# A four-layer graph kernel: how its first inputs arrive, and the order of its first products

## The chip, the cores and the metric

The kernel runs on one core of a Trainium2 chip. The metric is the device time of one execution in microseconds (us), the median of several. A core has a matrix engine (TensorE, PE), whose weight loads are shown apart (PEld), a vector engine (VectorE, DVE), a scalar engine (ScalarE, ACT), a general engine (GpSimd, POOL) and a sync engine (SP). Each engine works through its own list of instructions in order and waits for the others at semaphores. Transfers are issued by SP and by ACT, each on its own queue; both queues are served by the same 16 DMA engines. Matrix products are written to PSUM, eight banks of 128 x 512 numbers, and are read from there by DVE and ACT.

## What is computed

Four layers follow one another on 64 graphs of 128 nodes with 256 features. Each normalises its input, computes something of it and adds that to x:

```python
h = jnp.maximum(_layernorm(x, axis=-1), 0.0)
x = x + _L0_gnn_ref(h, adj, Wq, Wk, Wv)   # linear attention, relations normed by row
...                                       # L1: graph attention, L2: graph convolution, L3: 8-head attention

def _L0_gnn_ref(neuron_states, adjacency, Wq, Wk, Wv):
    q = jnp.einsum('bnd,ed->bne', neuron_states, Wq)
    k = jnp.einsum('bnd,ed->bne', neuron_states, Wk)
    v = jnp.einsum('bnd,ed->bne', neuron_states, Wv)
    rel = jnp.einsum('bnd,bmd->bnm', q, k)
    rel = adjacency.T[None, :, :] * rel
    rel = rel / jnp.linalg.norm(rel, axis=2, keepdims=True)
    return jnp.einsum('bnm,bmd->bnd', rel, v)
```

Only the first layer's start is touched here.

## The kernel before

All 64 graphs stay in on-chip memory (`xs`); the layers run one after the other, each over 32 pairs of graphs. In the first layer the two weights of query and key are multiplied once: q k^T is h (Wq^T Wk) h^T, so one product of the weights, `MM`, replaces two per pair. Each 32-bit operand of the large products is split into a rounded high part (written by ACT) and the rest, the low part (written by DVE from PSUM and the high part), and a product is the sum of high x high, high x low and low x high; such a `split_product` for one pair is 12 matmuls (L410).

The order on each engine is written out by hand, first a prologue, then `step(p, b)` for each pair. For one pair the work goes: moments, mean and variance (DVE L135 to L150, `statistics`), the reciprocal root (POOL L161), the normalised pair (`normalise` on DVE L706 for pairs 0 and 1, POOL from pair 2), its transposes on PE (`turn`, L172, into bank HT), high part on ACT (`relu_high`, L613 and L569), low part on DVE (`low_part`, L749), the t product with the split weights (`t_product`, L410, needs the low part), the values with the split value weight (`values`, L410; it needs the value bank to be read out by `low_v` of the pair before, DVE L766), `relation` (L494), the mask on DVE (L756), `relation_outputs` (L441) and the update of x (L773).

The prologue before: SP issues Wq, the second pair of graphs (2 and 3), Wv, the adjacency, W1, a small vector, the fifth pair and five weights of later layers. ACT issues the first pair (0 and 1, 256 KB), Wk, the four graphs of pairs 2 and 3 (512 KB, `x_third`), three bias rows, beta and the two small vectors bq and bk, whose elements lie apart in memory. PE runs six matmuls on zeros (L515), the product of the weights (L519, x8 in the profile, since a 32-bit matmul shows as two records), the first pair's transposes, the turn of Wv (L501), `t_product(0)`, `turn(1)`, the adjacency's transpose, `values(0)`, `relation(0)` and the turn of W1. On DVE the product of the weights is split by one subtraction of 128 x 512 (L783) and the turned Wv by another (L788); `degrees` sums the adjacency's rows.

Of the kernel before, what the change touches and what calls it, by code (L numbers as in the profile page):

```python
# [7 lines left out]
F32 = mybir.dt.float32  # L8
F32R = mybir.dt.float32r
ALU = mybir.AluOpType  # L10
# [4 lines left out]
def gnn_stack_kernel(nc, x, adj, w):  # L15

    GRAPHS, N, D = x.shape
# [11 lines left out]
    with ExitStack() as ctx:  # L30
# [3 lines left out]
        def sem(name):  # L34
            return ctx.enter_context(nc.semaphore(name))
# [133 lines left out]
        def transposes(pe_ps, src=xn):  # L169
            for c in range(C):  # L170
                for g in range(2):
                    ins = nc.tensor.transpose(pe_ps[:, c * 2 * N + g * N:c * 2 * N + (g + 1) * N],  # L172
                                              src[:, g, c * 128:(c + 1) * 128], ident[:, :])
            return ins
# [24 lines left out]
        qk_loaded, wv_loaded, w1_loaded, adj_loaded = sem("c_qk_loaded"), sem("c_wv_loaded"), sem("c_w1_loaded"), sem("c_adj_loaded")  # L199
        rows_loaded = sem("c_rows_loaded")  # L200
        raw_loaded = [sem(f"c_raw_loaded{k}") for k in range(5)]
        c_plain = sem("c_plain")
        c_zeros, c_ident, c_mhalf = sem("c_zeros"), sem("c_ident"), sem("c_mhalf")
        m_done, turned, wa_done, adjT_done = sem("c_m_done"), sem("c_turned"), sem("c_wa_done"), sem("c_adjT_done")
        plain_adjT_done = sem("c_plain_adjT_done")
# [11 lines left out]
        def chunks(weight):  # L217
            return weight.rearrange("(c p) n -> p c n", p=128)

        def as_chunks(ps):  # L220
            return ps[:, :].rearrange("p (c n) -> p c n", c=C)
# [205 lines left out]

        HT, TT, VV, RR, RT, OO = bank[0:6]
        AP = OO
        plain = wide[:, 0, 0:3, :].rearrange("p i n -> p (i n)")  # L430

        l0_v_ready, l0_relm_low, l0_out_done = v_ready, relm_low, out_done
# [12 lines left out]
        with nc.Block() as block:  # L445
            @block.sync
            def _(sp):
                sp.dma_start(wq0[:, :, :], chunks(w["L0_gnn_Wq"])).then_inc(qk_loaded, 16)
                sp.dma_start(xs[:, 2:4, :], x[2:4, :, :].rearrange("g n d -> n g d")).then_inc(x_second, 16)
                sp.dma_start(wv0[:, :, :], chunks(w["L0_gnn_Wv"])).then_inc(wv_loaded, 16)  # L450
                sp.dma_start(adj_sb[:, :], adj).then_inc(adj_loaded, 16)
                sp.dma_start(w1[:, :, 0:D], chunks(w["L1_gnn_W"])).then_inc(w1_loaded, 16)
                with nc.allow_non_contiguous_dma("columns of small vectors"):
                    sp.dma_start(a12[:, :, :].rearrange("p k c -> p (k c)"),
                                 w["L1_gnn_a"].rearrange("(k p) o -> p (k o)", p=128)).then_inc(w1_loaded, 16)
                sp.dma_start(xs[:, 2 * FIRST:2 * FIRST + 2, :],
                             x[2 * FIRST:2 * FIRST + 2, :, :].rearrange("g n d -> n g d")).then_inc(x_loaded, 16)
                for k, name in enumerate(("L2_gnn_weight", "L3_gnn_Wq", "L3_gnn_Wk", "L3_gnn_Wv", "L3_gnn_Wo")):
                    sp.dma_start(raw[k][:, :, :], chunks(w[name])).then_inc(raw_loaded[k], 16)
                with sp.Fori(FIRST + 1, PAIRS) as p:  # L460
                    sp.wait_ge(x_loaded, 16 * (p - FIRST))
                    sp.dma_start(x_pair(p), x[bass.ds(2 * p, 2), :, :].rearrange("g n d -> n g d")).then_inc(x_loaded, 16)

            @block.tensor
            def _(pe):
                def turn(p, b):
                    pe.wait_ge(xn_ready, p + 1)
                    pe.wait_ge(hT_ready, since(p))
                    transposes(HT, xnb[b]).then_inc(tr_done, 1)
# [8 lines left out]
                def t_product(p, b):  # L478
                    pe.wait_ge(low_ready, p + 1)
                    feature_product(TT, m_qk, hTs_of[b]).then_inc(t_done, 1)  # L480
# [17 lines left out]
                def turn_weight(ps, src):  # L498
                    for c in range(C):
                        for e in range(C):  # L500
                            ins = nc.tensor.transpose(ps[:, c * D + e * 128:c * D + (e + 1) * 128],  # L501
                                                      src[:, e, c * 128:(c + 1) * 128], ident[:, :])
                    ins.then_inc(turned, 1)
# [10 lines left out]
                for _ in range(6):  # L514
                    nc.tensor.matmul(OO[:, 0:D], plain[:, 0:128], plain[:, 128:128 + D], start=True, stop=True)  # L515
                pe.wait_ge(qk_loaded, 32)
                for d in range(C):
                    for e in range(C):
                        ins = nc.tensor.matmul(MM[:, d * D:(d + 1) * D], wq0[:, e, d * 128:(d + 1) * 128],  # L519
                                               wk0[:, e, :], start=(e == 0), stop=(e == C - 1))  # L520
                ins.then_inc(m_done, 1)
                pe.wait_ge(c_ident, 1)
                pe.wait_ge(xn_ready, 1)
                transposes(HT).then_inc(tr_done, 1)
                pe.wait_ge(wv_loaded, 16)
                turn_weight(WV, wv0)
                t_product(0, 0)
                turn(1, 1)
                pe.wait_ge(adj_loaded, 16)
                nc.tensor.transpose(AP[:, 0:N], adj_sb[:, :], ident[:, :]).then_inc(plain_adjT_done, 1)  # L530
                pe.wait_ge(wv_low, 1)
                values(0, 0)
                relation(0, 0)
                pe.wait_ge(w1_loaded, 32)
                turn_weight(W1, w1)
# [29 lines left out]
            def _(act):  # L565
# [32 lines left out]
                    act.wait_ge(raw_loaded[k], 16)  # L598
                    nc.scalar.copy((w2, wq3, wk3, wv3, wo3)[k][0][:, :, :], raw[k][:, :, :]).then_inc(w_high, 1)

                act.dma_start(xs[:, 0:2, :], x[0:2, :, :].rearrange("g n d -> n g d")).then_inc(x_first, 16)
                act.dma_start(wk0[:, :, :], chunks(w["L0_gnn_Wk"])).then_inc(qk_loaded, 16)
                act.dma_start(xs[:, 4:2 * FIRST, :], x[4:2 * FIRST, :, :].rearrange("g n d -> n g d")).then_inc(x_third, 16)
                for k, name in enumerate(("L2_gnn_bias", "L3_gnn_bv", "L3_gnn_bo")):
                    act.dma_start(rows[:, k, :], w[name].rearrange("(o n) -> o n", o=1).to_broadcast([128, D])).then_inc(rows_loaded, 16)
                act.dma_start(beta[:, :], w["L1_gnn_beta"].rearrange("(o n) -> o n", o=1).to_broadcast([128, 1])).then_inc(rows_loaded, 16)
                with nc.allow_non_contiguous_dma("columns of small vectors"):
                    act.dma_start(bq[:, :], w["L3_gnn_bq"].rearrange("(c p) -> p c", p=128)).then_inc(rows_loaded, 16)
                    act.dma_start(bk[:, :], w["L3_gnn_bk"].rearrange("(c p) -> p c", p=128)).then_inc(rows_loaded, 16)
                act.wait_ge(m_done, 1)  # L610
                nc.scalar.copy(m_qk[0][:, :, :], as_chunks(MM)).then_inc(c_high, 1)
                act.wait_ge(tr_done, 1)
                nc.scalar.activation(hT_high, HT[:, :], ACT.Relu).then_inc(high_ready, 1)  # L613
                act.wait_ge(turned, 1)
                nc.scalar.copy(wv0T[0][:, :, :], as_chunks(WV)).then_inc(c_high, 1)
                act.wait_ge(low_ready, 1)
# [76 lines left out]
            def _(dve):  # L693
# [75 lines left out]
                def update(p):  # L769
                    dve.wait_ge(rn_ready, p + 1)  # L770
                    dve.wait_ge(out_done, p + 1)
                    for g in range(2):
# [2 lines left out]
                    ins.then_inc(x_done, 1)  # L775

                nc.vector.memset(plain, 0.0).then_inc(c_plain, 1)
                dve.wait_ge(x_first, 16)
                statistics(0, 0)
                normalise(0)  # L780
                statistics(1, 1)
                dve.wait_ge(c_high, 1)
                nc.vector.tensor_tensor(m_qk[1][:, :, :], as_chunks(MM), m_qk[0][:, :, :].bitcast(F32), ALU.subtract)  # L783
                low_part(0, 0)
                normalise(1)
                degrees()
                dve.wait_ge(c_high, 2)
                nc.vector.tensor_tensor(wv0T[1][:, :, :], as_chunks(WV), wv0T[0][:, :, :].bitcast(F32),  # L788
                                        ALU.subtract).then_inc(wv_low, 1)
                statistics(2, 0)  # L790
                low_part(1, 1)
                dve.wait_ge(plain_adjT_done, 1)
# [894 lines left out]
```

## Time and profile before

| | us |
|---|---|
| median of 3 runs (lowest, highest) | 710.27 (710.08, 710.63) |
| the profiled execution, its own time | 710.56 |
| its span, first to last instruction | 708.8 |
| PE busy | 692.6 |
| DVE busy | 602.2 |
| ACT busy | 582.2 |
| POOL busy | 459.9 |

The granted clock of TensorE is 1.00 throughout. The page also gives the chain of work that ended last: followed back from the last instruction, at each step to what released it. Times of rows are counted from the first instruction. An instruction's duration runs until its result is there; the next one on its engine can start a little before, so that the distance of two starts is what a row costs its engine.

### The profile page before, as it was taken

Reading aid. Unit: us, or ns where it says so; the run is one execution under the profiler, and the core shown is the slowest. Engines: PE = TensorE matmul, PEld = TensorE weight load, DVE = VectorE, ACT = ScalarE, POOL = GpSimd, SP = SyncE. Lnnn points to the kernel's source line nnn. Section 1 sums busy time; section 2 is a strip of 40 time slices with the busy share of each in tenths; the row PEclk is TensorE's granted clock in tenths of the full one; section 3 lists DMA queues with packets and bytes.
Section 4 is the critical chain, followed back from the end, with each engine's and each line's share of the span. In section 5 each row is a group of like instructions: output and inputs, shape, how many; then the busy total and the mean of one; then the engine's idle time right before and its main releaser. Section 6 shows DMA issues by size and latency. Waiting matters only on the chain.

```text
span 708.8 us, 22691 instructions
## 1 busy us (share of the span) xinstructions
PE 692.6 (98%) x6950; PEld 653.8 (92%) x6950; DVE 602.2 (85%) x2523; ACT 582.2 (82%) x2023; POOL 459.9 (65%) x581
## 2 busy tenths in 40 slices
PE   8999999999999999999998999999999999999997
PEld 7999999999788888889997999999999999999995
DVE  6898988886488888699998998989888988898876
ACT  3787778777699999876665998889888988898896
POOL 2455656463477677578884776776677667766762
PEclk9999999999999999999999999999999999999999
DMA  8333210000000000000000000000000000000001
GB/s 249 91 90 90 89 30 0 0 0 2 0 2 1 2 1 2 1 2 0 0 0 1 17 32 18 30 30 24 21 30 30 20 25 30 30 16 30 32 32 45
DMA packets 21708, 20.29 MB, mean 29 GB/s; under 512 B 2448, under 2 KB 21648, under 8 KB 21648
## 3 DMA queue, kind: packets, MB, share of 16 engines
q1 hardware_dynamic: 19456, 18.16, 8.1%
q10 hardware_dynamic: 2192, 1.44, 0.7%
q8 instruction: 24, 0.39, 0.2%
q14 instruction: 36, 0.29, 0.1%
HBM read 11.21 MB, written 8.39 MB: 28 GB/s over the span
## 4 chain that ended last, share of the span: by engine, by line
PE 90%; ACT 4%; DVE 3%; issue 2%; POOL 1%; POOLq 0%; ACTq 0%; DVEq 0%
PE bank L410 43%; PE bank L1296 8%; PE bank L400 7%; PE bank L172 5%; PE bank L1288 5%; PE bank L1319 4%; PE bank L494 4%; PE bank L856 3%; PE bank L441 3%; PE bank L390 3%; PE bank L475 1%; PE bank L894 1%; PE bank L869 1%; ACT prob L1406 1%; PE bank L515 1%
## 5 line engine op out<-in xcount | busy, mean ns | idle before, releaser
L1406 ACT ACTIVATE prob<-wide,small 128x128 f32<-128x128 f32 x504 | 195.5, 392 | 2.1 <-DVE small L1532 2.1
L1488 POOL TENSOR_TENSOR prob<-prob,small 128x512 f32<-128x512 f32 x126 | 131.2, 1042 | 97.1 <-DVE small L1546 97.0
L1532 DVE CUSTOM_DVE_ANT_0 wide<-bank,mbias 128x128 f32<-128x128 f32 x512 | 115.1, 286 | 0.4 <-issue 0.4
L1406 ACT ACTIVATION_READ_ACCUMULATOR prob<-wide,small 128x1 f32 x504 | 95.7, 190 | 0.0
L1296 PE MATMUL bank<-ident,prob 128*128 128x128 f32 x504 | 71.1, 273 | 3.2 <-POOL prob L1488 2.9
L161 POOL TENSOR_TENSOR rstd<-vare,mhalf 128x2 f32<-128x2 f32 x88 | 61.6, 700 | 16.8 <-DVE vare L150 16.5
L659 POOL TENSOR_TENSOR rnorm<-norm,mhalf 128x2 f32<-128x2 f32 x32 | 22.3, 696 | 74.1 <-ACT relsq L594 74.1
L135 DVE BATCH_NORM_STATS2 stats<-xs 128x6 f32<-128x256 f32 (+1 forms) x176 | 65.5, 414 | 4.2 <-DMA xs<-in_x_dram 3.3
L247 POOL TENSOR_SCALAR xn<-xs,nmean,rstd 128x256 f32<-128x256 f32 x120 | 65.4, 555 | 5.5 <-POOL rstd L161 5.3
L1433 ACT COPY probT<-bank 128x512 f32<-128x512 f32 x94 | 50.9, 574 | 15.8 <-PE bank L1296 15.8
L400 PE MATMUL bank<-w,hT 128*128 128x258 f32 x256 | 61.5, 383 | 1.2 <-DVE oTs L766 1.1
L1296 PEld LDWEIGHTS bank<-ident,prob 128*128 128x128 f32 x504 | 57.4, 140 | 4.4 <-POOL prob L1488 3.9
L1008 POOL TENSOR_TENSOR xs<-xs,exp_u 128x512 f32<-128x512 f32 x32 | 40.9, 1277 | 29.5 <-DVE att L1060 27.4
L172 PE MATMUL bank<-ident,xn 128*128 128x128 f32 x376 | 56.3, 272 | 0.3 <-POOL xn L362 0.3
L410 PE MATMUL bank<-w,yTs 128*128 128x256 f32 x384 | 52.9, 286 | 2.5 <-DVE xs L311 2.2
L410 PE MATMUL bank<-hTs,wq 128*128 128x256 f32 x384 | 53.8, 289 | 0.6 <-DVE hTs L1550 0.6
L410 PE MATMUL bank<-hTs,wk 128*128 128x256 f32 x384 | 53.2, 288 | 0.0
L410 PE MATMUL bank<-wv,hTs 128*128 128x256 f32 x384 | 53.0, 287 | 0.0
L400 PEld LDWEIGHTS bank<-w,hT 128*128 128x128 f32 x256 | 46.2, 190 | 7.1 <-issue 1.3
L410 PEld LDWEIGHTS bank<-w,yTs 128*128 128x128 f32 x384 | 47.0, 188 | 4.8 <-DVE yTs L305 2.8
L410 PEld LDWEIGHTS bank<-hTs,wq 128*128 128x128 f32 x384 | 47.3, 188 | 4.4 <-DVE hTs L1550 0.8
L410 PE MATMUL bank<-wo,oTs 128*128 128x256 f32 x384 | 50.7, 281 | 0.2 <-DVE oTs L1588 0.2
(182 smaller groups left out, 1960.5 us busy)
## 6 DMA issues: line engine op xcount, KB each, us to landing
out_dram<-xs SPq DMA_DIRECT2D x31, 256.0 KB, 2.1
xs<-in_x_dram SPq DMA_DIRECT2D x29, 256.0 KB, 2.7
xs<-in_x_dram ACTq DMA_DIRECT2D x1, 512.0 KB, 7.4
xs<-in_x_dram ACTq DMA_DIRECT2D x1, 256.0 KB, 3.8
wq<-in_L_gnn_Wq_dram SPq DMA_DIRECT2D x1, 256.0 KB, 3.4
wk<-in_L_gnn_Wk_dram ACTq DMA_DIRECT2D x1, 256.0 KB, 4.7
wv<-in_L_gnn_Wv_dram SPq DMA_DIRECT2D x1, 256.0 KB, 5.8
w<-in_L_gnn_W_dram SPq DMA_DIRECT2D x1, 256.0 KB, 7.1
```

What stands on the lines that cost most here:

```text
L135: ins = nc.vector.bn_stats(stats[:, b, g, :], x_of(p, g))
L161: nc.gpsimd.tensor_tensor(rstd[:, b, :], vare[:, b, :], mhalf[:, 0:2], ALU.pow).then_inc(rstd_ready, 1)
L172: ins = nc.tensor.transpose(pe_ps[:, c * 2 * N + g * N:c * 2 * N + (g + 1) * N], src[:, g, c * 128:(c + 1) * 128], ident[:, :])
L247: ins = nc.gpsimd.tensor_scalar(xnb[b][:, g, :], x_of(p, g), nmean[:, b, g:g + 1], rstd[:, b, g:g + 1], ALU.add, ALU.mult)
L400: ins = nc.tensor.matmul(ps_g, hT[:, c, g, :], weight[:, c, :], start=(c == 0), stop=(c == C - 1))
L410: ins = nc.tensor.matmul(ps, lhsT(a, c), rhs(b, c), start=(n == 0), stop=(n == len(terms) - 1))
L1008: nc.gpsimd.tensor_tensor(x_pair(p), x_pair(p), exp_u[p % 2][:, :, :], ALU.add).then_inc(added, 1)
L1296: ins = nc.tensor.transpose(PT[r % 2][:, i * N:(i + 1) * N], prob[:, r, i, :], ident[:, :])
L1406: ins = nc.scalar.activation(prob[:, r, i, :], wide[:, r, i, :], ACT.Exp, bias=nmax[r][:, i:i + 1], scale=-1.0, accum_out=rsum[r][:, i:i + 1])
L1433: nc.scalar.copy(prob_turned[b][r], PT[r % 2][:, :].rearrange("p (i n) -> p i n", n=N)).then_inc(pt_ready, 1)
L1488: nc.gpsimd.tensor_tensor(prob[:, r, :, :], prob[:, r, :, :], rinv[r].unsqueeze(2).to_broadcast([128, QUAD, N]), ALU.mult).then_inc(prob_r ...
L1532: nc.vector.tensor_tensor_reduce(out=wide[:, r, i, :], in0=SS[r][:, i * N:(i + 1) * N], in1=mbias[:, :], scale=-1.0, scalar=3e38, op0=ALU. ...
```

## The change

The first pair comes by two transfers of one graph each, graph 1 at the head of SP's queue and graph 0 at the head of ACT's; both add to one semaphore. The transfer of the four graphs of pairs 2 and 3 moves from the third place of ACT's queue to the last, behind the small vectors. The product of the weights is made in two halves in two banks, one before and one after the first pair's transposes, each with its own high part on ACT and low part on DVE, and a new semaphore (`m_low`) that `t_product(0)` waits for. On DVE the second pair's statistics are broken up: moments early, mean, variance and root argument after the second half's low part. `values(0)` now stands ahead of `turn(1)`, and accordingly the low part of the turned Wv ahead of `normalise(1)`.

```diff
             def _(sp):
+                sp.dma_start(xs[:, 1, :], x[1, :, :]).then_inc(x_first, 16)
                 sp.dma_start(wq0[:, :, :], chunks(w["L0_gnn_Wq"])).then_inc(qk_loaded, 16)
...
+        query_key_bank = [MM, RR]
...
-                for d in range(C):
+                def query_key(d):
                     for e in range(C):
-                        ins = nc.tensor.matmul(MM[:, d * D:(d + 1) * D], wq0[:, e, d * 128:(d + 1) * 128],
+                        ins = nc.tensor.matmul(query_key_bank[d][:, 0:D], wq0[:, e, d * 128:(d + 1) * 128],
                                                wk0[:, e, :], start=(e == 0), stop=(e == C - 1))
-                ins.then_inc(m_done, 1)
+                    ins.then_inc(m_done, 1)
+
+                query_key(0)
                 pe.wait_ge(c_ident, 1)
                 pe.wait_ge(xn_ready, 1)
                 transposes(HT).then_inc(tr_done, 1)
+                query_key(1)
                 pe.wait_ge(wv_loaded, 16)
                 turn_weight(WV, wv0)
+                pe.wait_ge(m_low, 1)
                 t_product(0, 0)
-                turn(1, 1)
                 pe.wait_ge(adj_loaded, 16)
                 nc.tensor.transpose(AP[:, 0:N], adj_sb[:, :], ident[:, :]).then_inc(plain_adjT_done, 1)
                 pe.wait_ge(wv_low, 1)
                 values(0, 0)
+                turn(1, 1)
                 relation(0, 0)
...
-                act.dma_start(xs[:, 0:2, :], x[0:2, :, :].rearrange("g n d -> n g d")).then_inc(x_first, 16)
+                act.dma_start(xs[:, 0, :], x[0, :, :]).then_inc(x_first, 16)
                 act.dma_start(wk0[:, :, :], chunks(w["L0_gnn_Wk"])).then_inc(qk_loaded, 16)
-                act.dma_start(xs[:, 4:2 * FIRST, :], x[4:2 * FIRST, :, :].rearrange("g n d -> n g d")).then_inc(x_third, 16)
...
                     act.dma_start(bk[:, :], w["L3_gnn_bk"].rearrange("(c p) -> p c", p=128)).then_inc(rows_loaded, 16)
-                act.wait_ge(m_done, 1)
-                nc.scalar.copy(m_qk[0][:, :, :], as_chunks(MM)).then_inc(c_high, 1)
+                act.dma_start(xs[:, 4:2 * FIRST, :], x[4:2 * FIRST, :, :].rearrange("g n d -> n g d")).then_inc(x_third, 16)
+                def query_key_high(d):
+                    act.wait_ge(m_done, d + 1)
+                    nc.scalar.copy(m_qk[0][:, d, :], query_key_bank[d][:, 0:D]).then_inc(c_high, 1)
+
+                query_key_high(0)
                 act.wait_ge(tr_done, 1)
                 nc.scalar.activation(hT_high, HT[:, :], ACT.Relu).then_inc(high_ready, 1)
+                query_key_high(1)
...
-                dve.wait_ge(x_first, 16)
+                dve.wait_ge(x_first, 32)
                 statistics(0, 0)
                 normalise(0)
-                statistics(1, 1)
-                dve.wait_ge(c_high, 1)
-                nc.vector.tensor_tensor(m_qk[1][:, :, :], as_chunks(MM), m_qk[0][:, :, :].bitcast(F32), ALU.subtract)
+                def query_key_low(d):
+                    dve.wait_ge(c_high, d + 1)
+                    return nc.vector.tensor_tensor(m_qk[1][:, d, :], query_key_bank[d][:, 0:D], m_qk[0][:, d, :].bitcast(F32),
+                                                   ALU.subtract)
+
+                query_key_low(0)
+                dve.wait_ge(x_second, 16)
+                moments(dve, 1, dstep, 1)
                 low_part(0, 0)
+                query_key_low(1).then_inc(m_low, 1)
+                mean_variance(dve, 1, dstep, 1)
+                root_argument(dve, 1, dstep, stats_ready, 1)
+                dve.wait_ge(c_high, 3)
+                nc.vector.tensor_tensor(wv0T[1][:, :, :], as_chunks(WV), wv0T[0][:, :, :].bitcast(F32),
+                                        ALU.subtract).then_inc(wv_low, 1)
                 normalise(1)
                 degrees()
-                dve.wait_ge(c_high, 2)
-                nc.vector.tensor_tensor(wv0T[1][:, :, :], as_chunks(WV), wv0T[0][:, :, :].bitcast(F32),
-                                        ALU.subtract).then_inc(wv_low, 1)
                 statistics(2, 0)
                 low_part(1, 1)
```

On the matrix engine, around `turn(1)`: before, the four transposes of the second pair (`xn2`) and that of the adjacency stood between `t_product(0)` (`m_qk`) and `values(0)` (`wv0T`, first of its 12 rows here).

```order
L410 MATMUL bank<-hTs0,m_qk1 128x256
L172 MATMUL bank<-ident,xn2 128x128 [waits l0_hT_ready,l0_xn_ready]
L172 MATMUL bank<-ident,xn2 128x128 x3
L530 MATMUL bank<-ident,adj_sb 128x128 [waits c_adj_loaded]
L410 MATMUL bank<-wv0T0,hTs0 128x256 [waits l0_v_ready,c_wv_low]
```

The same engine now, from the product of the weights to the first row of `t_product(0)`.

```order
L521 MATMUL bank<-wk0,wq0 128x256 [waits c_qk_loaded]
L521 MATMUL bank<-wk0,wq0 128x256
L172 MATMUL bank<-ident,xn 128x128 [waits l0_xn_ready,c_ident]
L172 MATMUL bank<-ident,xn 128x128 x3
L521 MATMUL bank<-wk0,wq0 128x256 x2
L503 MATMUL bank<-ident,wv0 128x128 [waits c_wv_loaded]
L503 MATMUL bank<-ident,wv0 128x128 x3
L410 MATMUL bank<-hTs0,m_qk0 128x256 [waits l0_low_ready,c_m_low]
```

The first transposes moved ahead of half of the product, and `xn2` (no row of it here) moved behind all of `values(0)`, ahead of the first relation.

The vector engine before, from the statistics of pair 1 to those of pair 2 (rows of the statistics' small steps and second halves included):

```order
L142 BN_AGGR mv<-stats 128x2
L149 SCALAR_TENSOR_TENSOR nmean<-mv 128x2 [waits l0_dve_step]
L150 SCALAR_TENSOR_TENSOR vare<-mv 128x2
L783 TENSOR_TENSOR m_qk1<-bank,m_qk0 128x512 [waits c_high]
L749 SCALAR_TENSOR_TENSOR hTs1<-bank,hTs0 128x512 [waits l0_high_ready]
L706 TENSOR_SCALAR xn2<-xs,mv,rstd 128x256 [waits l0_rstd_ready]
L706 TENSOR_SCALAR xn2<-xs,mv,rstd 128x256
L712 TENSOR_REDUCE deg<-adj_sb 128x1 [waits c_adj_loaded]
L714 TENSOR_SCALAR deg<-deg 128x1 [waits c_deg_step]
L715 TENSOR_SCALAR deg<-deg 128x1
L788 TENSOR_TENSOR wv0T1<-bank,wv0T0 128x512 [waits c_high]
L135 BN_STATS stats<-xs 128x6 [waits l0_x_third]
```

And now:

```order
L793 TENSOR_TENSOR m_qk1<-bank,m_qk0 128x256 [waits c_high]
L142 BN_AGGR mv<-stats 128x2 [waits l0_dve_step]
L142 BN_AGGR mv<-stats 128x2
L149 SCALAR_TENSOR_TENSOR nmean<-mv 128x2 [waits l0_dve_step]
L150 SCALAR_TENSOR_TENSOR vare<-mv 128x2
L804 TENSOR_TENSOR wv0T1<-bank,wv0T0 128x512 [waits c_high]
L716 TENSOR_SCALAR xn2<-xs,mv,rstd 128x256 [waits l0_rstd_ready]
L716 TENSOR_SCALAR xn2<-xs,mv,rstd 128x256
L722 TENSOR_REDUCE deg<-adj_sb 128x1 [waits c_adj_loaded]
L724 TENSOR_SCALAR deg<-deg 128x1 [waits c_deg_step]
L725 TENSOR_SCALAR deg<-deg 128x1
L135 BN_STATS stats<-xs 128x6 [waits l0_x_third]
```

The low part of Wv moved ahead of `xn2` and the degrees; the statistics of pair 2, which wait for the moved transfer, still follow, directly behind the degrees.

## Rows read from the trace of the kernel before

**Rows 1.** The page: span, chain by engine, GB/s moved by 17.7 us slice.
```profile
span 708.8 us, 22691 instructions
...
GB/s 249 91 90 90 89 30 0 0 0 2 0 2 1 2 1 2 1 2 0 0 0 1 17 32 18 30 30 24 21 30 30 20 25 30 30 16 30 32 32 45
...
PE 90%; ACT 4%; DVE 3%; issue 2%; POOL 1%; POOLq 0%; ACTq 0%; DVEq 0%
```

**Rows 2.** The chain that ended last, 0 to 40 us: start, us, what.
```profile
6.81 1.84 PE bank L519 x8
...
10.64 1.68 PE bank L410 x12
12.32 0.44 PE bank L172 x4
...
12.87 1.42 PE bank L410 x12
...
15.61 1.41 PE bank L410 x12
```

**Rows 3.** Timeline to 10 us: start, us, engine, line, operation, out<-in, [idle before].
```profile
4.54 0.75 DVE L135 BATCH_NORM_STATS2 stats<-xs 128x6 f32<-128x256 f32 x2 [3.27 <-DMA xs<-in_x_dram]
...
6.82 0.73 DVE L706 TENSOR_SCALAR xn<-xs,mv,rstd 128x256 f32<-128x256 f32 x2 [0.90 <-POOL rstd L161]
...
9.15 0.60 ACT L613 ACTIVATE hTs<-bank 128x512 fp32r<-128x512 f32 x1
...
9.90 0.68 DVE L749 SCALAR_TENSOR_TENSOR hTs<-bank,hTs 128x512 fp32r<-128x512 f32 x1
```

**Rows 4.** Timeline of DVE, 10 to 23 us, the same columns.
```profile
10.50 0.73 DVE L706 TENSOR_SCALAR xn<-xs,mv,rstd 128x256 f32<-128x256 f32 x2
...
11.59 0.68 DVE L788 TENSOR_TENSOR wv0T<-bank,wv0T 128x512 fp32r<-128x512 f32 x1
12.19 0.74 DVE L135 BATCH_NORM_STATS2 stats<-xs 128x6 f32<-128x256 f32 x2
...
13.48 0.69 DVE L749 SCALAR_TENSOR_TENSOR yTs<-bank,yTs 128x512 fp32r<-128x512 f32 x1
...
15.62 0.42 DVE L756 TENSOR_TENSOR relm<-bank,adjT 128x256 f32<-128x256 f32 x1
15.95 0.68 DVE L766 TENSOR_TENSOR oTs<-bank,oTs 128x512 fp32r<-128x512 f32 x1
...
16.95 0.68 DVE L727 COPY w1T<-bank 128x512 f32<-128x512 f32 x1
18.18 0.69 DVE L749 SCALAR_TENSOR_TENSOR hTs<-bank,hTs 128x512 fp32r<-128x512 f32 x1 [0.55 <-ACT hTs L569]
...
21.25 0.88 DVE L773 SCALAR_TENSOR_TENSOR xs<-bank,rnorm,xs 128x256 f32<-128x256 f32 x2 [0.44 <-issue]
22.05 0.68 DVE L766 TENSOR_TENSOR oTs<-bank,oTs 128x512 fp32r<-128x512 f32 x1
```

**Rows 5.** Timeline: values(1) and values(2) on PE, a 256-wide copy on ACT.
```profile
17.43 1.67 PE L410 MATMUL bank<-wv0T,yTs 128*128 128x256 f32 x12
...
18.03 0.38 ACT L588 CAST rels<-bank 128x256 fp32r<-128x256 f32 x1
...
22.79 1.69 PE L410 MATMUL bank<-wv0T,hTs 128*128 128x256 f32 x12
```

**Rows 6.** Timeline: two issues on ACT's queue.
```profile
1.80 0.49 ACTq L603 DMA_DIRECT2D xs<-in_x_dram  x1
...
5.05 0.56 ACTq L609 DMA_DIRECT2D bk<-in_L_gnn_bk_dram  x1
```

**Rows 7.** DMA issues: out<-in, queue, KB each, median us from issue to landing.
```profile
xs<-in_x_dram ACTq DMA_DIRECT2D x1, 512.0 KB, 7.4
...
bk<-in_L_gnn_bk_dram ACTq DMA_DIRECT2D x1, 1.0 KB, 9.6
```

**Rows 8.** Waits of 20 to 100 us: engine, line, waited for, us, times, longest.
```profile
PEld bank L410 <- DVE oTs L766: 0.2, 1, 0.2
```

More of the change, by code:

```diff
@@ L201, in gnn_stack_kernel @@
         raw_loaded = [sem(f"c_raw_loaded{k}") for k in range(5)]
-        c_plain = sem("c_plain")
+        c_plain, m_low = sem("c_plain"), sem("c_m_low")
         c_zeros, c_ident, c_mhalf = sem("c_zeros"), sem("c_ident"), sem("c_mhalf")
```

## The prediction

> **What bounds the kernel now.** I read the page first [rows 1]: span 708.8 us, TensorE on 90% of the chain that ended last. So I read the chain of the start [rows 2], to see until when something other than TensorE decides. Its last such stretch ends at 10.64 us, where the first t product (x12) begins; from there to 40 us every piece of the chain is TensorE's. The waits of 20 to 100 us hold one wait of the matrix side, 0.2 us for VectorE's low part of the values [rows 8]; it belongs to values(2) [rows 5]. TensorE never idles in between, so whatever lead or lag it has after values(2) is carried to the end one to one: later stages are handed over by chains that start from TensorE's own last product. The change touches nothing later, so its whole effect is TensorE's shift at values(2), which starts at 22.79 us.
>
> The profiled execution took 710.56 us (span 708.8 plus 1.8 around it), 0.29 over the median 710.27. I work with shifts, which hold for either; the prediction is given against the median.
>
> **First pair by two transfers.** VectorE waited for it until 4.54 and had normalised it (6.82, 0.73) at 7.55 [rows 3]. Two loads of 128 KB side by side come at 4.54 at the latest and perhaps 0.7 us before. This buys nothing: the transposes now stand behind half of the query-key product, 6.81 + 1.84/2 = 7.73 [rows 2], later than 7.55. Cost and gain 0, covered by that half.
>
> **Query-key product in halves.** PE: half to 7.73, first transposes 0.44 to 8.17 (before: 8.65 to 9.09), second half to 9.09, weight turns to 9.53. ACT: high half from 7.75, 256 wide as in [rows 5], 0.38, to 8.15; relu of the turned pair from 8.21, 0.60 [rows 3], to 8.81; second high half at 9.5. DVE: a 256-wide subtraction from PSUM takes 0.42 and lets the next start after 0.33 (15.62 to 15.95, [rows 4]). So: low half 8.15; moments of pair 1 from 8.49, about 0.68, to 9.17; low part of h, 0.60 to the next start (9.90 to 10.50, [rows 3, 4]), until 9.77; second low half 9.77 + 0.42 = 10.19. The new wait on it starts the t product at 10.24 instead of 10.64. **Term 1: -0.40 us.** What is queued behind that wait on TensorE is everything, but it is the earlier end all the same. The second pair gets 128 KB more ahead of it on its queue; it had landed by 7.47, and at half of 249 GB/s [rows 1] 128 KB are 1.05 us: 8.5, just in time. The pieces are nine ACT DMA issues as before and one more on SP (0.5 us), all hidden.
>
> **Values ahead of the second turns.** The weight's low part: 9.77 + 0.34, the rest of the pair's statistics (1.29 - 0.68 = 0.61, [rows 4]) until 10.72, plus 0.68 = 11.40, before TensorE wants it (10.24 + 1.68 + 0.11 = 12.03). So values(0) runs 12.03 to 13.45 and the turns come at 13.45 to 13.89, where they stood 1.68 behind the t product's start before. TensorE's work from the first t product to the second is unchanged: 15.61 - 10.64 = 4.97 [rows 2], so it is free at 15.21. But VectorE's low part of pair 1 needs those turns and ACT's relu: 13.89 + 0.04 + 0.60 = 14.53, against 13.48 before [rows 4]. TensorE then starts the second t product at 14.53 + 0.74 = 15.27 (before 15.37 by its own rows, one matmul filling behind the other; its end moves from 17.02 to 16.93). **VectorE is now 1.05 us later** and has in its queue, in order: low part, adjT copy, statistics of pair 3 (13.48 to 15.62 in all), the mask, low_v(0) (0.33 later), adjacency and w1T (1.00), low part of pair 2. Late by 1.12 with the ends worked out: mask(0) 16.74, low_v(0) 17.07 to 17.75, w1T 18.07, low part of pair 2 at 18.68, where 0.55 us of idle time [rows 4] absorbs half of it: +0.50. values(1) started at 17.43 [rows 5]; it needs low_v(0), now 17.80. **Term 2: TensorE is +0.37 there**, so term 1 is gone and 0.37 more. values(2) needs low_v(1), 22.05 + 0.68 = 22.73 before. With VectorE +0.50 it starts at +0.50; if the 0.44 idle for issue ahead of the update at 21.25 [rows 4] doesn't recur, TensorE decides, at +0.37 less the 0.17 that it waited there: +0.20. Ends of term 2 with term 1 in it: **+0.20 to +0.50**, taken 0.35.
>
> **Third transfer last on ACT's queue.** It is issued at about 5.05 instead of 1.80 [rows 6]. It landed at 1.80 + 7.4 = 9.2 [rows 7], long before use. Statistics of pair 2 need it; their place is now after normalise and degrees (11.59 - 10.50 = 1.09, [rows 4]), which begin when POOL's root is there, at most 0.90 after the arguments [rows 3]: 10.72 + 0.90 + 1.09 = 12.7. They last 1.29 and the low part of pair 1 can't start before 14.53, so a landing up to 14.53 - 1.29 = 13.24 is free; each us past it delays everything by one. No row shows this landing. Lower bound: as long from issue as before, 5.05 + 7.4 = 12.45 [rows 7]. Upper: as long as the last request of the queue took, 5.05 + 9.6 = 14.65 [rows 6, 7], or 15 with some more. Middle: the queue holds the same requests less 128 KB and was empty at 14.65; at half of 249 GB/s these are 1.05 us, at the fastest rate about 0.5, so 13.6 to 14.1. I take 13.8, since this counts the work of the whole queue. **Term 3: 13.8 - 13.24 = +0.56** (0 to 1.4, 1.8 at 15).
>
> The Trainium skill ("DMA: Bandwidth & Descriptors", section "Queues, rings and completion order") says that on each DMA engine one queue's descriptors are taken in ring order, and its "Rules for kernel authors" that a strided last dimension costs one descriptor per element. By it the two small vectors, whose 1 KB each took up to 9.6 us to land [rows 7], stand wholly ahead of the 512 KB, which speaks against the change. No row here shows big data behind them on that queue; the sum by this rule would be that of rival C.
>
> **Sum.** 0.35 + 0.56 = +0.9 us: 710.27 + 0.9 = 711.2 (profiled execution 711.5).
>
> **Rivals.**
> A (forecast): the third transfer lands between 13.2 and 14.3, +0.2 to +1.5. For: the queue's total. 711.2. Chance 0.48.
> B: it lands before 13.24. For: the cheaper start of the queue; 12.45 is possible. Only term 2 is left, +0.20 to +0.50: 710.6. Chance 0.18.
> C, slower: the small requests hold up the 512 KB behind them on some engine, landing behind 14.3, about 15. It decides from 13.24 on; 15.0 - 13.24 = 1.76, plus 0.35 = +2.1: 712.4. For: the last vector took 9.6 us, two more than the 512 KB. Against: part of this was 640 KB more ahead of it. Chance 0.20.
> D, gain: the turns' delay costs VectorE less than the rows give (its queue runs closer than I add up), no new wait forms, and TensorE keeps term 1 plus the 0.17: -0.40 to -0.57, 709.8. For: TensorE is the bound everywhere behind 10.64. Against: 1.05 us of lateness on VectorE meets only 0.8 us of slack at low_v(0) (16.63 against 17.43). Chance 0.14.
>
> **Numbers.** 0.2% is 1.42 us, about what a measurement of this kernel can tell from no change. D is capped at -0.57, so faster needs something outside these cases: 0.03. Slower takes C and a little of A's top: 0.22. Within: 0.75. The range 709.9 to 712.5 leaves out half of D below and the tail of C above.
>
> **What the profile after would show.** The first t product's start at 10.24 (term 1); low part of pair 1 at 14.5 or later on VectorE; a wait of values(1) on low_v(0) that was not there, with values(1) starting at 17.8 plus whatever term 3 is; VectorE's statistics of pair 2 waiting for the DMA past 12.7 (A, C) or not (B); values(2) at 22.79 plus the total. It would be wrong if the statistics of pair 2 find their data at 12.7 and values(1) doesn't wait, or if something past 40 us changes, such as TensorE waits in the first layer that [rows 8] doesn't have.

## The result, and the profile after

The changed kernel takes 714.05 us (median of 5 runs, 712.99 to 715.21) against 710.08 (709.79 to 710.63): ratio 1.0055, 95% interval 1.0044 to 1.0066. That is +3.97 us where +0.9 was forecast, beyond the upper end of the range, 712.5. It also spreads over 2.2 us, the kernel before over 0.8. The profiled execution is the lowest of the five, 712.99 with a span of 711.2; against the trace of the kernel before (710.56, span 708.8) that is +2.4. Of the other 1.6 us, 0.5 is there because the profiled execution before lay above its median, and 1.1 because this one lies below its own. No trace shows those 1.1 us.

The page of the changed kernel: span, busy time, granted clock, chain by engine. TensorE is as long busy as before (692.5); DMA and ACT's queue stand in the chain now with 1% each, where [rows 1] had no DMA and 0% of ACT's queue.

```profile
span 711.2 us, 22695 instructions
...
PE 692.5 (97%) x6950; PEld 652.9 (92%) x6950; DVE 598.0 (84%) x2524; ACT 582.9 (82%) x2024; POOL 461.0 (65%) x581
...
PEclk9999999999999999999999999999999999999999
...
PE 87%; ACT 3%; DVE 3%; issue 2%; POOL 1%; DMA 1%; ACTq 1%; POOLq 0%; DVEq 0%
```

The chain that ended last, its first 27 us (start, us, what). Before, it was TensorE's from 10.64 on [rows 2]. Now it runs over ACT's issues to the moved transfer, which lands 9.15 us after its issue, and on over VectorE to `values(1)` at 19.80:

```profile
5.51 0.56 ACTq L614
6.11 9.15 DMA xs<-in_x_dram
15.28 0.76 DVE stats L135 x2
...
16.65 0.60 DVE yTs L759
17.25 0.20 DVE adjT L811
17.45 0.67 DVE stats L135 x2
...
18.81 0.33 DVE relm L766
19.15 0.61 DVE oTs L776
19.75 0.04 issue
19.80 1.68 PE bank L410 x12
```

VectorE's timeline, to set beside [rows 3, 4]. Its idle stretches stand in brackets: the first low half comes at 8.59, not at 8.15, and the statistics of pair 2 wait 2.27 us for the DMA, with 13.01 to 15.28 empty.

```profile
3.50 0.75 DVE L135 BATCH_NORM_STATS2 stats<-xs 128x6 f32<-128x256 f32 x2 [2.24 <-DMA xs<-in_x_dram]
...
8.59 0.42 DVE L793 TENSOR_TENSOR m_qk<-bank,m_qk 128x256 fp32r<-128x256 f32 x1 [2.08 <-ACT m_qk L618]
...
15.28 0.75 DVE L135 BATCH_NORM_STATS2 stats<-xs 128x6 f32<-128x256 f32 x2 [2.27 <-DMA xs<-in_x_dram]
```

ACT's timeline to 9 us. The issue of beta took 1.45 us and that of bq 0.80, where each took about 0.5 before; the moved transfer is therefore issued at 6.11 (forecast 5.05), the table load follows at 6.89, and the first high half, whose operand TensorE had finished by about 6.9, starts at 8.19. SP's queue stalls in the same stretch, its W1 issue from 3.19 for 1.44.

```profile
3.20 1.45 ACTq L611 DMA_DIRECT2D beta<-in_L_gnn_beta_dram  x1
4.68 0.80 ACTq L613 DMA_DIRECT2D bq<-in_L_gnn_bq_dram  x1
5.51 0.56 ACTq L614 DMA_DIRECT2D bk<-in_L_gnn_bk_dram  x1
6.11 0.76 ACTq L615 DMA_DIRECT2D xs<-in_x_dram  x1
6.89 1.28 ACT L618 ACT_TABLE_LOAD   x1 [6.89 <-issue]
8.19 0.37 ACT L618 CAST m_qk<-bank 128x256 fp32r<-128x256 f32 x1
```

TensorE: the first t product at 10.65, the second at 17.31 after 1.69 us of idle time, `values(2)` at 25.02.

```profile
10.65 1.68 PE L410 MATMUL bank<-hTs,m_qk 128*128 128x256 f32 x12 [1.55 <-DVE m_qk L793]
...
17.31 1.66 PE L410 MATMUL bank<-yTs,m_qk 128*128 128x256 f32 x12 [1.69 <-DVE yTs L759]
...
25.02 1.67 PE L410 MATMUL bank<-wv0T,hTs 128*128 128x256 f32 x12
```

`values(2)` stood at 22.79 before [rows 5]: +2.23 there, and the span is 2.4 longer. So nearly all of this execution's loss is made in the first 25 us and carried to the end.

### The profile page after: what moved, and what is told of

The parts are those of the page before. It is cut to its first block, busy times and chain, and to the rows that moved or that the text cites. A ratio compares the mean times of both kernels' runs of the same rounds, so it can differ in the third digit from the quotient of the medians.

```text
span 711.2 us, 22695 instructions
## 1 busy us (share of the span) xinstructions
PE 692.5 (97%) x6950; PEld 652.9 (92%) x6950; DVE 598.0 (84%) x2524; ACT 582.9 (82%) x2024; POOL 461.0 (65%) x581
## 4 chain that ended last, share of the span: by engine, by line
PE 87%; ACT 3%; DVE 3%; issue 2%; POOL 1%; DMA 1%; ACTq 1%; POOLq 0%; DVEq 0%
PE bank L410 43%; PE bank L1314 8%; PE bank L400 7%; PE bank L172 5%; PE bank L1306 5%; PE bank L1337 4%; PE bank L496 4%; PE bank L874 3%; PE bank L442 3%; PE bank L390 3%; DMA xs<-in_x_dram 1%; PE bank L477 1%; PE bank L912 1%; PE bank L887 1%; ACT prob L1424 1%
```

## The experiments

Theory T: the late third transfer costs the time. Rival R: it is the order, values ahead of the second turns. Two more came up on the way: the value weight's landing, and ACT's table load behind its issues. All ratios are against the kernel before on the same chip, whose median there was 710.26 (experiments 1, 2, 4 to 7) or 710.16 (3, 8, 9). Each profile is of one execution.

**1. The third transfer back in third place**, the rest as changed.

```diff
                 act.dma_start(wk0[:, :, :], ...)
+                act.dma_start(xs[:, 4:2 * FIRST, :], ...).then_inc(x_third, 16)
...
                     act.dma_start(bk[:, :], ...)
-                act.dma_start(xs[:, 4:2 * FIRST, :], ...).then_inc(x_third, 16)
```

> The changed kernel with one part undone: the transfer of pairs 2 and 3 is back in third place of ACT's queue; split first pair, halved product and values ahead of turn(1) stay. Theory T (the late third transfer costs the time): its landing is near 9 us, VectorE's statistics of pair 2 start at about 12.7 without a DMA wait, values(2) starts at 22.8 to 23.3, time +0.2 to +0.6 against the kernel before, 710.3 to 710.7, and the wide spread of the changed kernel's runs is gone. Rival R (the order values before turns, which makes VectorE late, costs it): 712.5 to 714 as the changed kernel.

Measured: 711.54 (12 runs, 710.34 to 713.65), ratio 1.0019 (1.0010 to 1.0028). 2.5 us of the loss are gone and 1.3 stay, more than T wanted, and so does a spread of 3 us. Its profile is of its lowest run (span 708.6, 0.2 below the kernel before), so it does not show where the 1.3 go. In it no statistics wait for data, and TensorE waits instead for the value weight:

```profile
9.15 0.66 PE L503 MATMUL bank<-ident,wv 128*128 128x128 f32 x4 [0.94 <-DMA wv<-in_L_gnn_Wv_dram]
9.64 1.69 PE L410 MATMUL bank<-hTs,m_qk 128*128 128x256 f32 x12
...
17.15 1.69 PE L410 MATMUL bank<-wv0T,yTs 128*128 128x256 f32 x12
```

Here the t product starts 1.0 us before the 10.64 of [rows 2]. But 0.8 of this is an earlier start of the product of the weights, at 5.78 against 6.61 in the timeline before, since TensorE's warm-up lasted 4.57 us and not 5.49. `values(1)` starts only 0.3 before its 17.43: 0.7 us are lost in the stretch where the order differs. Experiment 6 has that order alone.

**2. The third transfer alone, in the kernel before.**

```diff
                 act.dma_start(wk0[:, :, :], ...)
-                act.dma_start(xs[:, 4:2 * FIRST, :], ...).then_inc(x_third, 16)
...
                     act.dma_start(bk[:, :], ...)
+                act.dma_start(xs[:, 4:2 * FIRST, :], ...).then_inc(x_third, 16)
```

> The kernel before with one part of the change alone: the transfer of pairs 2 and 3 last on ACT's queue. Theory T: it lands at 14.7 to 15.3 or later, the statistics of pair 2 (12.19 before) wait for it, the low part of pair 1 follows 1.29 behind it, values(2) is 2 to 3 us late, time 712 to 713.5 with a wide spread. Rival R: 710.1 as before.

Measured: 715.42 (5 runs, 714.24 to 716.76), ratio 1.0065 (1.0052 to 1.0078). This one part costs +5.2 us, more than the whole change. The profile is of its slowest run, 716.76. The statistics wait 4.36 us, to 16.62, TensorE idles 3.05 us, and the next twelve matmuls take 2.93 us instead of 1.66:

```profile
16.62 0.75 DVE L135 BATCH_NORM_STATS2 stats<-xs 128x6 f32<-128x256 f32 x2 [4.36 <-DMA xs<-in_x_dram]
```
```profile
18.65 2.93 PE L410 MATMUL bank<-yTs,m_qk 128*128 128x256 f32 x12 [3.05 <-DVE yTs L749]
```

```profile
15.00:18.00 3.00, 0.60 (x6) 0.36 (x4) 1.24 (x7) 0.00 (x0) 0.00 (x0) 0.99 0.60 197
18.00:20.00 2.00, 1.35 (x6) 1.35 (x7) 1.86 (x8) 1.08 (x2) 1.73 (x3) 0.50 0.08 9
20.00:22.00 2.00, 2.00 (x11) 2.00 (x10) 2.00 (x8) 0.39 (x1) 0.77 (x2) 0.50 0.42 131
22.00:24.00 2.00, 2.00 (x12) 2.00 (x11) 0.98 (x3) 1.73 (x8) 0.01 (x1) 0.50 0.47 131
```

The Trainium skill, page "TensorE: Matmul & The Clock Gate", section "Why this matters for your kernels", says that idle gaps between bursts of matmuls bring the clock back to its lower level; this trace agrees, with 0.50 behind 3.05 us of idle time.

**3. The same, with work in the gap.**

```diff
                 turn_weight(W1, w1)
+                for _ in range(5):
+                    nc.tensor.matmul(RT[:, 0:D], plain[:, 0:128], plain[:, 128:128 + D], start=True, stop=True)
```

> The kernel before with the transfer of pairs 2 and 3 last on ACT's queue (which alone took 715.42, its profile with a granted clock of 0.50 from 18 to 24 us behind 3 us without matmuls), plus five matmuls on zeros into an unused bank between the turn of W1 and the second t product, 2 us of work in that idle time. If the fall of the clock behind the idle stretch is a part of the cost of its own, the granted clock stays at 1.00 and the time falls by 1.5 to 2.5 us to 713 to 714 with more work done. If only the late landing counts, 715.4 or more.

Measured: 714.07 (4 runs, 713.99 to 714.20), ratio 1.0053 (1.0037 to 1.0068), 1.3 us less than without the five matmuls, though a little less than was expected, and the spread shrinks from 2.5 to 0.2 us. The data came nearly as late (the statistics start at 16.28, 0.34 earlier), the idle rest is 0.46 us, and the clock holds:

```profile
15.00:18.00 3.00, 2.85 (x17) 2.24 (x15) 1.58 (x7) 0.00 (x0) 0.27 (x1) 1.00 0.62 201
18.00:20.00 2.00, 1.69 (x14) 1.69 (x15) 1.86 (x9) 1.07 (x2) 1.65 (x4) 1.00 0.29 59
```

So of the +5.2 about +3.9 are the wait itself and some 1.3 the clock behind it, and the clock made most of the spread in this kernel. The runs of experiment 2 say the same: the one with a mean granted clock of 1.000 took 714.24, like this kernel, and the one with 0.995 took 716.76.

**4. What holds the third transfer up?** First, between the bias rows and the small vectors:

```diff
                     act.dma_start(rows[:, k, :], ...)
+                act.dma_start(xs[:, 4:2 * FIRST, :], ...).then_inc(x_third, 16)
                 act.dma_start(beta[:, :], ...)
```

> The changed kernel with the transfer of pairs 2 and 3 behind the three bias rows but ahead of beta, bq and bk, the requests with small elements. If the small requests ahead of it hold the data up, it lands at about 11.5 us, inside what VectorE leaves free (13.2), and the time is that of the third place, 710.3 to 710.7. If the bytes ahead of it or its late issue are what counts, it lands at 13.5 or later and the time is 711 to 713.

Measured: 712.29 (5 runs, 712.04 to 714.40), ratio 1.0041 (1.0028 to 1.0054). It landed 10.4 us after an issue at 3.20, at 13.6, by its expectation the sign of bytes ahead and not of small elements. But no one waited for it, since everything ahead was late too: the value weight came at 10.9 and the table load ended at 8.98. The profiled run is one of three with a clock of 1.000 (712.04 to 712.29); the other two have 0.998 and take 713.95 and 714.40.

```profile
10.89 0.65 PE L503 MATMUL bank<-ident,wv 128*128 128x128 f32 x4 [2.22 <-DMA wv<-in_L_gnn_Wv_dram]
```
```profile
4.74 1.45 ACTq L614 DMA_DIRECT2D bq<-in_L_gnn_bq_dram  x1
6.22 1.45 ACTq L615 DMA_DIRECT2D bk<-in_L_gnn_bk_dram  x1
7.70 1.28 ACT L618 ACT_TABLE_LOAD   x1 [7.70 <-issue]
```

Then behind the small vectors but ahead of the rows, the order being beta, bq, bk, third transfer, rows:

> The changed kernel with the three bias rows behind the transfer of pairs 2 and 3, which is then behind beta, bq and bk only. If the rows are what holds it up, it lands at 10 to 12 us, inside what is free, and the time is that of the third place, about 711.5. If the small elements hold it up, it lands at 13 or later and takes 712 or more.

Measured: 711.62 (10 runs, 711.09 to 713.93), ratio 1.0020 (1.0011 to 1.0030), as experiment 1. In its profile, which is of its slowest run (713.93), the transfer was issued at 3.23 and landed 8.9 later, at 12.1, and no statistics waited. So either group ahead of it alone, 640 small elements or 384 KB of rows, delays it (third in the queue it lands at 8.2 to 9.9), but not beyond what VectorE leaves free; both together do.

This profile also shows the clock falling at another place. The table load ended at 9.26 and the value weight came late (its turn starts at 9.67), so that from 8.15 to 11.74 TensorE worked only the 0.66 us of the weight's turn. Its clock was then at 0.50 until 15.0, and the first t product took 2.93 us:

```profile
9.67 0.66 PE L503 MATMUL bank<-ident,wv 128*128 128x128 f32 x4 [1.52 <-DMA wv<-in_L_gnn_Wv_dram]
11.74 2.93 PE L410 MATMUL bank<-hTs,m_qk 128*128 128x256 f32 x12 [1.42 <-DVE m_qk L793]
```
```profile
12.00:14.00 2.00, 2.00 (x10) 2.00 (x11) 1.75 (x8) 0.00 (x0) 0.70 (x1) 0.50 1.04 332
```

Last, the rows at their place, but not one row of 1 KB read 128 times each:

```diff
-                    act.dma_start(rows[:, k, :], w[name].rearrange("(o n) -> o n", o=1).to_broadcast([128, D]))...
+                    act.dma_start(rows[:, k, :], x[60 + k, :, :])...
```

> The changed kernel, whose three bias rows come not from one row of 1 KB read 128 times each but from 128 different rows of x (so the biases are wrong values; bytes, count and place of the requests are the same). If reading one row 128 times slows the DMA engines, the issues on the queues no longer stall for 1 to 1.5 us from 3.2 us on, the DMA rate of 4 to 8 us rises from 290 to 350 GB/s, the moved transfer lands at 13.5 or earlier instead of 15.3, and the time falls from 714 to about 711.5. If not, 713 to 715.

Measured: 713.94 (4 runs, 713.04 to 714.47), ratio 1.0056 (1.0041 to 1.0072), like the changed kernel. The early stalls of the issues were away in its profile, of its lowest run (bq 0.52, bk 0.69, the transfer issued at 4.96 instead of 6.11), but it landed 10.4 us after, at 15.35. Reading the same row again is not the cause, and nor is the late issue: issued 1.15 us earlier, it landed at the same time. With ACT free sooner the first t product started 0.8 us before that of the changed kernel, and it bought nothing, since `values(2)` came at 25.09 (25.02):

```profile
9.86 1.67 PE L410 MATMUL bank<-hTs,m_qk 128*128 128x256 f32 x12 [0.76 <-DVE m_qk L793]
```

The landings (issue plus time to landing) show what counts. The moved transfer lands 2 to 3 us behind the request ahead of it on ACT's queue, whenever it was itself issued:

| run | request ahead | lands at | moved transfer lands at |
|---|---|---|---|
| changed kernel | bk | 12.2 | 15.3 |
| this one, distinct rows | bk | 12.4 | 15.4 |
| experiment 2 | bk | 13.8 | 16.6 |
| experiment 3 | bk | 13.3 | 16.3 |
| behind the rows only | third row | 10.5 | 13.6 |
| behind the small vectors only | bk | 10.0 | 12.1 |

**5. The first pair split, alone.**

> The kernel before with the first pair by two transfers alone. Its statistics start near 3.5 instead of 4.54 and nothing else moves, since the transposes wait for TensorE: 710.1, within 0.2. If the split is what makes the issues on both queues stall for 1.45 us at 3.2 us, as the changed kernel's trace shows, the table load on ACT ends near 8.2 instead of 6.9, the high part of the product is late by some tenths only (8.67 before) and the time is 710.1 to 710.5.

Measured: 710.23 (11 runs, 709.46 to 712.45), ratio 1.0001 (0.9992 to 1.0010). Free on average, as the prediction had it, but with a spread of 3 us: in the profiled run (711.09) the value weight, which has 128 KB more ahead of it, landed at 10.6 (7.5 before) and the weight turn waited 1.66 us. Why 3 us later is not shown.

```profile
10.63 0.66 PE L502 MATMUL bank<-ident,wv 128*128 128x128 f32 x4 [1.66 <-DMA wv<-in_L_gnn_Wv_dram]
11.04 1.65 PE L410 MATMUL bank<-hTs,m_qk 128*128 128x256 f32 x12
```

**6. Values ahead of turn(1), alone.**

```diff
                 t_product(0, 0)
-                turn(1, 1)
...
                 values(0, 0)
+                turn(1, 1)
                 relation(0, 0)
```

> The kernel before with the third part alone: values(0) ahead of turn(1), and the weight's low part ahead of normalise(1). By term 2 without term 1: the low part of pair 1 near 14.9 instead of 13.5, low_v(0) 1.4 us later, values(1) at about 18.1 instead of 17.43: 710.6 to 711.2, with as little spread as the kernel before. If the order costs nothing: 710.2.

Measured: 710.86 (11 runs, 710.59 to 711.47), ratio 1.0011 (1.0002 to 1.0020): +0.6, where the mechanism of term 2 gives 0.3 to 0.9. In its profile the first t product started at 10.15, 0.49 earlier than before, because the warm-up (5.11 us) and the product of the weights (1.89) were shorter than before (5.49 and 2.03), and its `values(1)` at 17.63, 0.20 later than before: 0.7 us lost between the two, as in experiment 1.

**7. The halves and the split alone** (third transfer in third place, turn(1) ahead of the values).

> The changed kernel with two parts undone: the transfer of pairs 2 and 3 back in third place, and turn(1) back ahead of values(0), with VectorE's order of normalise(1), degrees and the weight's low part as before. What is left is the halved product and the split first pair. If the remaining 1.3 us of the run with the third place alone (711.54 against 710.26) come from the order values before turns, this one starts the first t product at 9.6 to 10.2, has no wait of values(1), and takes 709.4 to 710.2. If they come from the value weight landing late (9.1 in that run's profile, behind 128 KB more), it takes 710.8 to 711.6 and keeps a spread of over 1 us.

Measured: 711.39 (11 runs, 710.70 to 712.66), ratio 1.0017 (1.0008 to 1.0026): what was forecast as -0.4 is +1.1. In its profile (711.70) the table load starts at 6.92 and the t product at 10.68, no sooner than before; then turn(1) waits 0.31 for VectorE's normalised pair and `values(0)` 0.27 for the weight's low part, because the pair's mean and variance now stand behind the second low half:

```profile
12.66 0.66 PE L172 MATMUL bank<-ident,xn 128*128 128x128 f32 x4 [0.31 <-DVE xn L716]
...
13.70 1.68 PE L410 MATMUL bank<-wv0T,hTs 128*128 128x256 f32 x12 [0.27 <-DVE wv0T L806]
```

**8. The same with ACT's queue cut short**: bias rows, beta, bq and bk at the end of SP's queue.

> The run with the halved product and the split first pair alone (711.39), with the six requests for bias rows, beta, bq and bk moved from ACT's queue to the end of SP's. If the halves buy nothing because ACT is still issuing and loading its table (until 8.2 us there), the table load ends near 3.6 us, the first high part starts at 6.8 to 7.5, the first t product at 9.3 to 9.8, and the time is 709.9 to 710.6. If the value weight's landing or VectorE's order holds it, 711 or more.

Measured: 710.51 (10 runs, 710.19 to 711.00), ratio 1.0004 (0.9995 to 1.0013), 0.9 us less than experiment 7, in the range expected. The table load is done at 3.5 and the t product starts at 9.64:

```profile
2.21 1.28 ACT L618 ACT_TABLE_LOAD   x1 [2.21 <-issue]
7.17 0.37 ACT L618 CAST m_qk<-bank 128x256 fp32r<-128x256 f32 x1 [3.68 <-PE bank L527]
```

The first high half now waits for TensorE, and no longer for ACT. This shows that ACT's issues and table load held the halves back. But TensorE's two waits on VectorE are there again (0.30 and 0.27), and the earlier start is used up by `values(1)`: 17.49, 0.06 later than in [rows 5].

**9. Two tries at a faster kernel.** The first is experiment 8 with three more changes: Wv moves behind Wk on ACT's queue, the statistics of pair 1 stand whole ahead of the first low half, and the degrees stand behind the weight's low part. The second is the kernel before with the split first pair and the same queues and place of the degrees, without the halves.

> A try at a faster kernel: as the run before with, besides, Wv behind Wk on ACT's queue, VectorE's statistics of pair 1 whole and ahead of the first low half, and the degrees behind the weight's low part. First t product at 9.6, no wait of TensorE behind it, 709.0 to 709.8. If VectorE's chain still holds the second t product, 710.0 or more.

> The same without the halves: the kernel before with the split first pair, the six requests at the end of SP's queue, Wv on ACT's queue, the degrees behind the weight's low part. The product of the weights whole from about 5.9 or 6.6, first t product at 9.7 to 10.2, 709.0 to 709.8. If halving is worth something once ACT is free, this one is slower than the other by 0.2 or more.

Measured: with halves 709.74 (11 runs, 709.15 to 710.62), ratio 0.9993 (0.9984 to 1.0002); without 710.14 (11 runs, 709.33 to 713.01), ratio 1.0008 (0.9998 to 1.0017). The first may be 0.4 us faster than the kernel before, but its interval reaches 1; it takes 4 us less than the changed kernel. TensorE has no wait behind its first t product in either profile. In the first the t product came at 10.15, though, and not at the 9.6 expected, since VectorE now had the statistics first. The second was expected at 709.0 to 709.8 and missed that; that the halves are worth the 0.4 us between the two is not shown, as the intervals overlap. The second reached `values(1)` at 16.35 in its profile, 1.1 us before [rows 5], and 709.33, its lowest run; three of its eleven runs have a granted clock of 0.998 and take 711.6 to 713.0. No trace shows them, so where their clock fell stays open; experiment 4's second profile shows one place in this stretch where it can.

## Why the prediction was wrong, point by point

**The bound, and that a shift is carried to the end**: right. +2.23 at `values(2)`, +2.4 in the span, with no new wait of TensorE behind it.

**Term 1, -0.40 for the halves: failed.** The t product came at 10.65, not 10.24. The step that failed is "nine ACT DMA issues as before, all hidden": they took until 6.87 instead of 5.6, the table load of 1.28 us stands behind them, and the first high half needs ACT at 7.75 at the latest. Before, ACT had slack there, since the whole product ended at 8.65; the halves used that slack up. The size of the term was right where ACT is free. Counted from the start of the product of the weights, which moves with the warm-up, the t product came after 4.03 us before (6.61 to 10.64), 4.74 in the changed kernel (5.91 to 10.65) and 3.53 in experiment 8 (6.11 to 9.64), and 3.53 too in experiment 4's last. But in the trace of the changed kernel this failure is not what costs the time: once the data of pair 2 come last, the chain runs from their landing, and term 1 drops out of it.

**Term 2, +0.20 to +0.50**: right in its mechanism. The predicted times hold when the real landing is put in: the low part of pair 1 at 15.28 + 1.29 = 16.57 (measured 16.57), `values(1)` at 17.80 + (15.28 - 13.24) = 19.84 (measured 19.80). The wait on `low_v(0)` is the link that the chain shows. The 0.44 us of issue idle ahead of the update did not come back in this trace, which makes it the lower end of the term: 0.20 and the 2.04 of late data give 2.24, and `values(2)` was 2.23 late. Alone the order costs +0.6.

**Term 3, +0.56: mis-sized; this is what made the forecast wrong.** It measured 15.28 - 13.24 = 2.04. The landing was put at 13.8, with 15 as the far end; it was 15.28 in the lowest run, 15.35 in experiment 4's last, 16.28 and 16.62 with the third transfer alone. The step that failed is "the queue holds the same requests less 128 KB and was empty at 14.65", which took the time to empty the queue as a measure of its bytes. In the old order the last row on ACT's queue had landed at 10.5, and the 4.1 us from there to 14.65 went by with nothing but beta, bq and bk left on it, while the DMA engines moved 186 and then 368 GB/s, nearly all for SP's queue:

```profile
10.00:12.00 2.00, 1.36 (x11) 1.36 (x12) 1.97 (x7) 0.84 (x2) 0.25 (x1) 1.00 0.75 186
12.00:14.00 2.00, 2.00 (x19) 2.00 (x18) 1.86 (x8) 1.09 (x2) 0.67 (x2) 1.00 1.08 368
```

In the new order the last row landed at 8.7 and bk at 12.2, 3.5 us that did not shrink much, and the 512 KB then took another 3.1 behind it instead of running beside or ahead of it:

```profile
bk<-in_L_gnn_bk_dram ACTq DMA_DIRECT2D x1, 1.0 KB, 6.7
```
```profile
8.00:10.00 2.00, 0.89 (x6) 0.42 (x4) 1.41 (x4) 1.80 (x5) 0.00 (x0) 1.00 0.76 170
```

It is not that the engines moved less. They have a slow stretch here too, 170 GB/s from 8 to 10 us, as the 186 from 10 to 12 before, and up to 16 us both kernels moved 4.23 MB (the stretches' GB/s times their length). So rival C was the case that came true, given 0.20: its mechanism, small requests that hold up the 512 KB behind them, and its +2.1 at a landing of 15. Why a vector of 1 KB takes 6 to 10 us to land in this stretch is not shown.

**What no case had**: that a wait of this length costs TensorE's clock as well. In experiments 2 and 3 that was 1.3 us. In the changed kernel it is at most a small part of the median. The trace at hand is at 1.00, and so are four of the five runs, the median run (714.05) among them; a mean clock that rounds to 1.000 leaves at most 0.0005 x 712 = 0.4 us for it (an estimate). Only the slowest run, 715.21, has 0.998. So most of the 1.1 us between the trace and the median has another cause, later landings perhaps, which no trace shows.

**The rivals**: B and D did not occur. The sum of the single parts (third last +5.2, values first +0.6, halves with split +1.1) is more than the whole, +4.0. In the traces the statistics waited 4.36 us for the third transfer alone and 2.27 in the changed kernel. Of the difference, 1.34 is an earlier landing in the changed kernel (15.28 against 16.62), whose cause is open, and 0.75 is VectorE's place: it came to these statistics at 13.01 instead of 12.26, so that the late order left room for the late data. The clock behind the longer wait adds to the single part too.

Open are two things: why the issues on both queues stall together for 1 to 2 us, in the changed kernel's profile at 3.2 us and in experiment 5's at 5.1, and what the run at the median looked like.

## What to carry to other kernels

A transfer moved to the end of a queue lands behind the request ahead of it, here by 2 to 3 us for 512 KB. So price it as the landing of that request plus its own time, and not by when the old queue was empty: a queue whose last requests are vectors of small elements can be without bytes for microseconds while it waits for them. Then compare that with its consumer's place in the engine's order. Before an engine's work is pulled forward, look at what that engine still has in front: here DMA issues that can take three times their usual length, and a table load behind them. If a wait leaves TensorE idle for some microseconds, count the lower clock behind it as a cost of its own.

## What the runs showed of the hardware

The first five issues on ACT's or SP's queue took 0.4 to 0.6 us each in every trace; later ones took up to 2.6 us (the last weight on SP's queue in the kernel before), and where both queues still had requests to issue, the long ones mostly came on both at once (1.44 and 1.45 at 3.2 us, 2.23 and 2.27 at 5.1 us in experiment 5). The granted clock was 0.50 for 6 us after 3.05 us without matmuls, and for over 3 us after 3.6 us with 0.66 us of work in them (experiment 4's second profile); with 0.46 us of idle time left it stayed at 1.00. Three rows read 128 times each from one place took no longer than 384 different ones (713.94 against 714.05 us). A 512 KB transfer landed 2.1 to 3.1 us behind the request ahead of it where that was a bias row or bk. The same twelve warm-up records of TensorE lasted 4.3 to 5.5 us in the profiles of this case, and the product of the weights behind them started between 5.64 and 6.61: this alone moves what follows by a microsecond, so compare starts in two traces only after taking it off.
